# Moving the product that spreads the gates over rows to the bank of the first values, in the second cross attention of a two-layer gated block

## The chip, the cores and the metric

One core of a Trainium2 chip. The time is that of one execution on the device, in microseconds; the kernel before has a median of 4245.28 us over 3 runs (4242.39 to 4248.78).

## The reference

The program is a block of four parts on `x` (64 sequences of 64 rows of 128), in fp32. Each part adds its gated result to `x`; ahead of each stands a layer norm. The parts are a cross attention with memory slots, six layers of local attention and feed-forward, a second cross attention with gates, and a mixture of experts. The change lies in the third:

```python
attn = softmax(einsum('bhnd,bhmd->bhnm', q, k) * SCALE, axis=-1)
g = transpose(x @ w_la, (0, 2, 1))
gate = 0.5 * mean(g, axis=-1)[:, :, None, None] + 0.5 * max(g, axis=-1)[:, :, None, None]
attn2 = softmax(gate * attn, axis=-1)
attn = w * attn2 + (1.0 - w) * attn
out = einsum('bhnm,bhmd->bnhd', attn, v).reshape(B, N, C)
return out @ w_proj + b_proj
```

Here `x` is the context, and there are 16 heads of 8 columns. For each sequence and head there is one number `gate`. It multiplies a whole row of the first softmax, and what comes of that goes through a second softmax. Both softmaxes weigh the same values.

## The kernel before

The third part works on 32 tiles of 128 rows, two sequences each. It is a software pipeline: in one round an engine works for tile `a` on its projections, for `b` (the tile before) on its scores, for `c` on its first softmax, for `d` on its second, for `e_` on its second values and its output, and for `f` on the norm for the next part. Each engine runs its own list in program order (`l_body` in each engine's block), and semaphores tie the lists together. `past(engine, name, count)` makes an engine wait for a semaphore. TensorE, ScalarE, VectorE and GpSimd each have their own list. The names in the prediction:

- `turn(tile, k, h)`: four transpositions of half `h` of the exponentials, for the first (`k` = 0, into `pp`) or second softmax (`k` = 1, into `turn`). ScalarE copies them to SBUF (`l_C1`, `l_C2`), and `pv(tile, k)` multiplies them by the values into `po[k]`, 16 small products at line 1750, signalled by `l_P1` or `l_P2`. The 17th and 18th columns of each product are the sums of the softmax.
- The bank `pj[1]` is shared within a round by four things: the transposed inputs (`xsx`, line 1763), the turned sum `l_os` (line 1798), the projection by `lpj` (line 1802), and the gates' product (line 1811). Each has to wait until the reader of the one before is through.
- The gates' product: GpSimd writes the gates of a tile as rows that all hold the sequence's value (`l_gb`, signal `l_ga`, line 717), and TensorE multiplies them by the identity, so that each row gets the 16 gates of its sequence. VectorE multiplies them by the reciprocal of the softmax's sums (`l_c1`, line 1329), and GpSimd then multiplies the exponentials by them (the tile `qn`, line 739, signal `l_z`).
- VectorE adds the projection to `X` (line 1314, signal `l_res`), then takes the reciprocal, the maximum and sum of the next gates (`l_gm`), `l_c1`, and the second half of the subtraction of the first softmax (line 1264). Line 1334 writes the normalised `Y`.
- On GpSimd the sum of the weighted values (`oT`, line 721, waiting for VectorE's line 1278), the keys (`big`, line 727), the bias on `X` and the deviation (`rstd`) stand between one multiplication by the gates and the next.

Of the kernel before, what the change touches and what calls it, by code (L numbers as in the profile page):

```python
# [19 lines left out]
L1H, L1D = 16, 8  # L20
# [10 lines left out]
ALU = mybir.AluOpType  # L31
# [18 lines left out]
def build(nc, x, ctx, g_xattn, g_ffn, wq_w, wq_b, wk_w, wk_b, wv_w, wv_b, mk, mv, wo_w, wo_b,  # L50
# [3 lines left out]
    with ExitStack() as stack:  # L54
        def sb(name, shape, dt=F32):
            return stack.enter_context(nc.sbuf_tensor(name, shape, dt))
# [3 lines left out]
        def sem(name):  # L60
            if name not in sems:
                sems[name] = stack.enter_context(nc.semaphore(name))
            return sems[name]
# [7 lines left out]
        def const(name):  # L71
            a, n = CONSTS[name]
            return K[:, a:a + n]

        ident = const("ident")
# [81 lines left out]
        pj = [stack.enter_context(nc.psum_tensor(f"pj{i}", [P, 512], F32)) for i in range(2)]  # L157
# [3 lines left out]
        po = [stack.enter_context(nc.psum_tensor(f"po{i}", [P, 512], F32)) for i in range(2)]  # L161
# [45 lines left out]
        def bc(ap, n):  # L207
            return ap.unsqueeze(len(ap.shape)).broadcast_to(list(ap.shape) + [n])
# [30 lines left out]
        def by_head(v):  # L239
            return v.rearrange("p (j t) -> p j t", t=S)  # L240
# [10 lines left out]
        l_kq = [kT[:, 2 * i:2 * i + 2, :] for i in range(2)]  # L251
        l_pT = [[pT[:, h, :] for h in range(2)], [sqb[h] for h in range(2)]]
        l_out = [po[i][:, 0:144].rearrange("p (k c) -> p k c", c=18) for i in range(2)]
        l_gb = [oT[:, i, :] for i in range(2)]
        l_o1 = [oT[:, 2 + i, :] for i in range(2)]
        l_o2, l_os, l_oT = oT[:, 4, :], oT[:, 5, :], oT[:, 6, :]
# [3 lines left out]
        l_rc = sb("l_rc", [P, 2, L1H])  # L260
        l_rw = sb("l_rw", [P, 2, L1H])
        l_c1 = sb("l_c1", [P, 2, L1H])
# [18 lines left out]
        def past_waits(eng, name):  # L281

            eng.sem_inc(sem(name), 1)
# [98 lines left out]
        def head_start(eng, *names):  # L382

            for name in names:
                eng.sem_inc(sem(name), START)

        def past(eng, name, count):

            eng.wait_ge(sem(name), count + START)  # L389
# [189 lines left out]
        def _(pool):  # L579
            def rsqrt(i, n, name, count):  # L580

                nc.gpsimd.tensor_tensor(n_eps(i, n), n_var(i, n), eps1[:, 0:n], ALU.add).then_inc(sem(name), 1)
                past(pool, name, count + 1)
                nc.gpsimd.tensor_tensor(n_rstd(i, n), n_eps(i, n), nhalf[:, 0:n], ALU.pow).then_inc(sem(name), 1)
# [122 lines left out]
            def l_body(a, b, c, d, e_, f):  # L707
                if b:
                    k = b.par % 2
                    past(pool, "l_gs", b.g + 1)  # L710
                    nc.gpsimd.tensor_tensor(l_gm[:, k, :], l_gm[:, k, :], l_half[:, :], ALU.mult).then_inc(sem("l_g1"), 1)
                    pool.wait_ge(sem("l_g1"), b.g * 2 + 1)
                    nc.gpsimd.tensor_tensor(l_gm[:, k, 0:2], l_gm[:, k, 0:2], l_gm[:, k, 2:4], ALU.add).then_inc(sem("l_g1"), 1)
                    pool.wait_ge(sem("l_g1"), b.g * 2 + 2)
                    past(pool, "l_gr", b.g - 1)
                    past_waits(pool, "went_on")
                    nc.gpsimd.tensor_copy(l_gb[k].rearrange("p (b s) -> p b s", b=BT), bc(l_gm[:, k, 0:2], S)).then_inc(sem("l_ga"), 1)
                if e_:
                    past(pool, "l_t2", e_.g + 1)
                    past(pool, "l_oT", e_.g)  # L720
                    nc.gpsimd.tensor_tensor(l_os, l_o1[e_.par % 2], l_o2, ALU.add).then_inc(sem("l_os"), 1)
                if a:
                    past(pool, "l_kq", a.g + 1)
                    past(pool, "l_s", a.g - 1)
                    kk = l_kq[a.par % 2][:, 0, :].rearrange("p (b t) -> p b t", b=BT)
                    for bb in range(BT):
                        nc.gpsimd.tensor_tensor(l_km[a.par % 2][:, bb], kk[:, bb, :].unsqueeze(1).broadcast_to([P, L1HALF, S]),
                                                bc(const("headmask"), S), ALU.mult).then_inc(sem("l_km"), 1)
                if b:
                    nc.gpsimd.tensor_tensor(X[:, b.t, :], X[:, b.t, :], lpb[:, :], ALU.add).then_inc(sem("l_xb"), 1)  # L730
                if f:
                    past(pool, "norm_ag", f.g + (NT + NF + 1))
                    rsqrt(f.par, 1, "norm_nr", f.g * 2 + (2 * NT + 2 * NF))
                if c:
                    k = c.par % 2
                    past(pool, "l_c1", c.g + 1)
                    for h in range(2):
                        past(pool, "l_T2", c.g * 2 - 3 + h)
                        nc.gpsimd.tensor_tensor(by_head(l_e2[k][h]), by_head(l_e1[k][h]), bc(l_c1[:, k, L1HALF * h:L1HALF * h + L1HALF], S), ALU.mult).then_inc(sem("l_z"), 1)
# [5 lines left out]
            pool.wait_ge(sem("zeroed"), 3)  # L745
            pool.wait_ge(sem("l_la1"), 1)
            stream(pool, NT, l_body, 0, 0, 6, 4)


# [250 lines left out]
        def _(dve):  # L1000
# [253 lines left out]
            def l_body(a, b, c, d, e_, f):  # L1254
# [60 lines left out]
                if c:  # L1315
                    k = c.par % 2
# [7 lines left out]
                    nc.vector.tensor_reduce(l_gm[:, a.par % 2, 2:4], gv, AX, ALU.add).then_inc(sem("l_gs"), 1)  # L1324
                if c:
                    past(dve, "l_rc1", c.g * 2 + 1)
                    past(dve, "l_gr", c.g + 1)
                    past(dve, "l_z", c.g * 2 - 2)
                    nc.vector.tensor_tensor(l_c1[:, k, :], pj[1][:, 0:L1H], l_rc[:, k, :], ALU.mult).then_inc(sem("l_c1"), 1)
                    nc.vector.tensor_scalar(l_rw[:, k, :], l_rc[:, k, :], law[:, 1:2], None, ALU.mult).then_inc(sem("l_rc1"), 1)  # L1330
                sub1(1)
                if f:
# [91 lines left out]
        @block.tensor  # L1424
        def _(pe):
            mm = nc.tensor.matmul
            head_start(pe, "l_T", "l_pj", "l_s", "l_T1", "l_T2", "l_P1", "l_P2", "l_oT", "l_pr", "l_gr", "x_T", "x_ch", "x_s", "x_t", "x_pv", "x_wo", "d_xT", "d_ch", "d_vp", "d_tt", "d_s", "d_pt", "d_pv", "d_wo", "f_h", "f_y", "f_xnT")
            pe.wait_ge(s_ld, NLOAD)
            for i in range(2):
                if i:  # L1430
# [301 lines left out]
            def l_body(a, b, c, d, e_):  # L1732
# [9 lines left out]
                def pv(tile, k):  # L1742
                    if tile:
                        past(pe, "l_C%d" % (k + 1), tile.g * 2 + 2)
                        past(pe, "l_t%d" % (k + 1), tile.g)
                        past_waits(pe, "went_on")
                        for p in range(8):
                            for bb in range(BT):
                                q = slice(bb * 64, bb * 64 + 64)
                                last = mm(l_out[k][q, p, :], l_pT[k][p // 4][:, (p % 4) * P + bb * 64:(p % 4) * P + bb * 64 + 64],  # L1750
                                          l_vp[tile.par][:, bb, p, :], start=True, stop=True)
                        last.then_inc(sem("l_P%d" % (k + 1)), 1)
# [2 lines left out]
                turn(c, 0, 0)  # L1755
                if a:
                    pe.wait_ge(sem("l_in%d" % (a.par % 2)), a.half * 64 + (a.par // 2 * 32 + 32))
                    if d:
                        past(pe, "l_c1", d.g + 1)
                    else:  # L1760
                        past(pe, "l_xc", a.g)
                    for i in range(2):
                        last = nc.tensor.transpose(pj[1][:, i * P:i * P + P], xsx[:, a.par % 2, i, :], ident)
                    last.then_inc(sem("l_T"), 1)
# [25 lines left out]
                if e_:  # L1790
                    past(pe, "l_os", e_.g + 1)
                    if a:
                        past(pe, "l_xc", a.g + 1)
                    elif d:
                        past(pe, "l_c1", d.g + 1)
                    else:
                        past(pe, "l_res", e_.g)
                    nc.tensor.transpose(pj[1][:, 0:P], l_os, ident).then_inc(sem("l_oT"), 1)
                pv(c, 0)
                if e_:  # L1800
                    past(pe, "l_oc", e_.g + 1)
                    mm(pj[1][:, 0:D], l_oT, lpj[:, :], start=True, stop=True).then_inc(sem("l_pr"), 1)
                if c:
                    past(pe, "l_ga", c.g + 1)
                    if e_:
                        past(pe, "l_res", e_.g + 1)
                    elif a:
                        past(pe, "l_xc", a.g + 1)
                    else:
                        past(pe, "l_c1", c.g)  # L1810
                    mm(pj[1][:, 0:L1H], l_gb[c.par % 2][0:L1H, :], ident[0:L1H, 0:L1H], start=True, stop=True).then_inc(sem("l_gr"), 1)

            past(pe, "f_hT", DEPTH * (3 * NF))
            past(pe, "f_xT", DEPTH * NF)
# [118 lines left out]
```

## Time and profile before

| | us |
|---|---|
| median of 3 runs | 4245.28 |
| profiled execution | 4245.7 |
| its span, first to last instruction | 4243.9 |
| TensorE matmuls busy | 4020.4 (95%) |
| VectorE busy | 3504.6 (83%) |
| ScalarE busy | 2999.4 (71%) |
| GpSimd busy | 2867.3 (68%) |

The third part lies between about 3620 and 3997 us. Busy shares are means over the whole program and say little on one part, so the rows below are read in windows of that part. A timeline row gives the start in us from the span's beginning, the duration, engine, line, operation, what is written from what, and the count of merged instructions; a matmul in fp32 leaves two records.

### The profile page before, as it was taken

How to read it: one execution, taken by the hardware profiler on the slowest of the kernel's cores; microseconds unless marked ns; L12 is line 12 of the kernel's file. 1: busy time of each engine (PE TensorE's matmuls, PEld its weight loads, DVE VectorE, ACT ScalarE, POOL GpSimd, SP SyncE). 2: the span in 40 equal slices, each digit the busy share in tenths (PEclk: the TensorE clock that was granted, in tenths of full speed). 3: DMA queues.
4: the chain of work that ended last, by engine and by line, in shares of the span. 5: the costliest groups of instructions: out<-in, count | busy, mean ns of one | idle time of the engine just before them, and what ended most of it. 6: DMA issues, size and time to landing. Idle time of an engine off the chain costs nothing.

```text
span 4243.9 us, 147344 instructions
## 1 busy us (share of the span) xinstructions
PE 4020.4 (95%) x50345; PEld 2806.3 (66%) x50345; DVE 3504.6 (83%) x7236; ACT 2999.4 (71%) x6796; POOL 2867.3 (68%) x3647
## 2 busy tenths in 40 slices
PE   5999998999999999999999999999999998788799
PEld 3777775666666666666666666666666666566665
DVE  4666667999888998899988998899989998677566
ACT  2555556888888888788878887888888887554322
POOL 2333337888888888888887888788888887555200
PEclk9999999999999999999999999999999999887699
DMA  3000001000000001000000001000010000000000
GB/s 89 6 7 7 6 4 48 10 8 10 24 22 9 9 8 34 12 8 9 24 21 8 10 7 31 16 10 7 10 35 11 7 10 9 18 12 11 2 10 10
DMA packets 162227, 64.81 MB, mean 15 GB/s; under 512 B 121556, under 2 KB 156128, under 8 KB 162016
## 3 DMA queue, kind: packets, MB, share of 16 engines
q1 hardware_dynamic: 162016, 62.05, 5.8%
q8 instruction: 126, 2.06, 0.2%
q14 instruction: 85, 0.70, 0.1%
HBM read 26.54 MB, written 2.10 MB: 7 GB/s over the span
## 4 chain that ended last, share of the span: by engine, by line
POOL 43%; issue 25%; PE 24%; DVE 5%; POOLq 2%; SPq 1%; ACT 1%; DVEq 0%; DMA 0%; ACTq 0%
POOL qn L646 10%; POOL qn L635 8%; POOL big L646 7%; POOL e L641 5%; POOL big L635 4%; PE pj L1506 3%; PE pp L1464 2%; PE po L1479 2%; PE sc L1861 2%; PE pj L1498 2%; PE pj L1547 1%; POOL rstd L657 1%; PE po L1485 1%; POOLq L389 1%; PE turn L1450 1%
## 5 line engine op out<-in xcount | busy, mean ns | idle before, releaser
L1573 PE MATMUL pj<-wqkv,xcT 128*128 128x512 f32 x1536 | 799.5, 602 | 17.0 <-issue 9.2
L646 POOL TENSOR_TENSOR qn<-qn,big 128x512 f32<-128x512 f32 x384 | 490.5, 1278 | 289.9 <-DVE big L1139 289.9
L818 ACT ACTIVATE big<-pj 128x512 f32<-128x512 f32 x768 | 473.7, 617 | 69.0 <-PE pj L1573 59.2
L1139 DVE TENSOR_TENSOR big<-pj,ropes 128x512 f32<-128x512 f32 x768 | 521.3, 679 | 0.0
L1145 DVE TENSOR_REDUCE ss<-big 128x8 f32<-128x512 f32 x768 | 514.8, 671 | 0.1
L646 POOL TENSOR_TENSOR big<-big 128x512 f32<-128x512 f32 x384 | 485.1, 1273 | 4.7 <-DVE big L1139 4.7
L1726 PEld LDWEIGHTS pp<-wo,oT 128*128 128x128 f32 x3072 | 358.7, 192 | 161.7 <-issue 82.6
L641 POOL TENSOR_TENSOR e<-e,rc 128x512 f32<-128x512 f32 x384 | 400.2, 1042 | 55.7 <-DVE rc L1169 55.7
L635 POOL TENSOR_TENSOR qn<-qn,ny 128x512 f32<-128x512 f32 x384 | 396.7, 1043 | 7.5
L635 POOL TENSOR_TENSOR big<-big,ny 128x512 f32<-128x512 f32 x384 | 396.2, 1043 | 7.6
L1726 PE MATMUL pp<-wo,oT 128*128 128x128 f32 x3072 | 395.4, 282 | 2.3 <-ACT oT L841 1.2
L1580 PE MATMUL pj<-wqkv,xcT 128*64 128x512 f32 x1536 | 395.0, 614 | 0.7 <-DVE big L1139 0.6
L1138 DVE TENSOR_TENSOR qn<-pj,ropec 128x512 f32<-128x512 f32 x384 | 262.2, 683 | 134.5 <-ACT big L818 110.8
L861 ACT ACTIVATE e<-e 128x512 f32<-128x512 f32 x384 | 242.1, 631 | 116.5 <-DVE e L1158 114.4
L1138 DVE TENSOR_TENSOR big<-pj,ropec 128x512 f32<-128x512 f32 x384 | 263.6, 687 | 66.4 <-ACT big L818 60.2
L1663 PE MATMUL po<-f_xcT,fw 128*128 128x256 f32 (+1 forms) x1152 | 298.0, 382 | 1.5 <-DVE hT L1179 0.8
L1158 DVE TENSOR_TENSOR e<-sc,mx 128x512 f32<-128x512 f32 x384 | 265.5, 691 | 36.4
L1663 PEld LDWEIGHTS po<-f_xcT,fw 128*128 128x128 f32 (+1 forms) x1152 | 202.4, 180 | 114.5 <-issue 90.3
L1151 DVE TENSOR_REDUCE mx<-sc 128x8 f32<-128x512 f32 x384 | 260.4, 678 | 6.0 <-PE sc L1617 5.9
L1573 PEld LDWEIGHTS pj<-wqkv,xcT 128*128 128x128 f32 x1536 | 232.1, 191 | 45.6 <-DVE big L1139 27.2
L1163 DVE TENSOR_REDUCE sm<-e 128x8 f32<-128x512 f32 x384 | 259.4, 676 | 0.0
L612 POOL TENSOR_TENSOR e<-e,x_rc 128x384 f32<-128x384 f32 x128 | 105.7, 826 | 216.7 <-DVE x_rc L1064 216.7
(320 smaller groups left out, 9938.3 us busy)
## 6 DMA issues: line engine op xcount, KB each, us to landing
wqkv<-in_L_ffn_Wqkv SPq DMA_DIRECT2D x18, 512.0 KB, 3.7
xsd<-Y SPq DMA_DIRECT2D x192, 32.0 KB
xsd<-Y SPq DMA_DIRECT2D x384, 15.8 KB
xsf<-Y SPq DMA_DIRECT2D x96, 64.0 KB
xsf<-Y SPq DMA_DIRECT2D x192, 31.5 KB
xsx<-Y SPq DMA_DIRECT2D x64, 64.0 KB, 1.8
xsx<-CT SPq DMA_DIRECT2D x64, 64.0 KB, 1.9
wo<-in_L_ffn_Wo SPq DMA_DIRECT2D x6, 512.0 KB, 4.2
```

Of the source, the lines that this page charges most:

```text
L635: nc.gpsimd.tensor_tensor(uv, uv, bc(ny[:, tile.par, 8 * i:8 * i + 8], DK), ALU.mult).then_inc(sem("d_un"), 1)
L641: nc.gpsimd.tensor_tensor(ev, ev, bc(rc[:, p, 0:8], S), ALU.mult).then_inc(sem("d_pr"), 1)
L646: nc.gpsimd.tensor_tensor(U[a.par][i], U[a.par][i], t2b[i % 2], ALU.add).then_inc(sem("d_add"), 1)
L818: nc.scalar.activation(sqb[i % 2], pj[i % 2][:, :], ACT.Square).then_inc(sem("d_sq"), 1)
L1138: nc.vector.tensor_tensor(t1v, pv, cos, ALU.mult)
L1139: nc.vector.tensor_tensor(t2v, swapped, sin, ALU.mult).then_inc(sem("d_r"), 1)
L1145: nc.vector.tensor_reduce(ss[:, i, :], sqb[i % 2].rearrange("p (h d) -> p h d", d=DK), AX, ALU.add).then_inc(sem("d_ss"), 1)
L1158: nc.vector.tensor_tensor(e[:, p, :].rearrange("p (a t) -> p a t", t=S), sv, bc(mx[:, p, 0:8], S), ALU.subtract).then_inc(sem("d_sub"), 1)
L1573: mm(pj[i % 2][:, :], xcT[:, a.par, :], wqkv[:, i * 512:i * 512 + 512], start=True, stop=True).then_inc(sem("d_ch"), 1)
L1580: last = mm(pj[bb][a2 * 64:a2 * 64 + 64, :].rearrange("p (q c) -> p q c", c=2 * DK), xcT[:, a.par, bb * 64:bb * 64 + 64], wv[:, a2], start ...
L1663: last = mm(f_hid[j][0:m, (1 - k) * 256:(1 - k) * 256 + 256], fw1[:, k * FI + o:k * FI + o + m], f_xcT[:, :], start=True, stop=True)
L1726: last = mm(pp[:, 0:D], oT[:, k, :], wo[:, k, :], start=(k == 0), stop=(k == HP - 1))
```

## The change

The gates' product no longer goes to `pj[1]` at the end of a round but to 16 free columns of `po[0]`, directly ahead of the 16 products of the first values. It has no signal of its own (`l_gr` is gone): VectorE relies on `l_P1`, that of the values. Two waits are added at the head of the values, for `l_ga` and for `l_c1` of the tile before. The inputs' transpositions now wait for `l_res` of the last finished tile, as that is what last reads `pj[1]`. GpSimd waits for `l_P1` before it overwrites a gates buffer.

```diff
+        l_gates = po[0][:, 144:144 + L1H]
...
-                    past(pool, "l_gr", b.g - 1)
+                    past(pool, "l_P1", b.g - 1)
...
                     past(dve, "l_rc1", c.g * 2 + 1)
-                    past(dve, "l_gr", c.g + 1)
                     past(dve, "l_z", c.g * 2 - 2)
-                    nc.vector.tensor_tensor(l_c1[:, k, :], pj[1][:, 0:L1H], l_rc[:, k, :], ALU.mult).then_inc(sem("l_c1"), 1)
+                    nc.vector.tensor_tensor(l_c1[:, k, :], l_gates, l_rc[:, k, :], ALU.mult).then_inc(sem("l_c1"), 1)
...
                         past(pe, "l_C%d" % (k + 1), tile.g * 2 + 2)
                         past(pe, "l_t%d" % (k + 1), tile.g)
+                        if k == 0:
+                            past(pe, "l_ga", tile.g + 1)
+                            past(pe, "l_c1", tile.g)
                         past_waits(pe, "went_on")
+                        if k == 0:
+                            mm(l_gates, l_gb[tile.par % 2][0:L1H, :], ident[0:L1H, 0:L1H], start=True, stop=True)
                         for p in range(8):
...
-                    if d:
-                        past(pe, "l_c1", d.g + 1)
+                    if e_:
+                        past(pe, "l_res", e_.g)
                     else:
                         past(pe, "l_xc", a.g)
...
                     if a:
                         past(pe, "l_xc", a.g + 1)
-                    elif d:
-                        past(pe, "l_c1", d.g + 1)
                     else:
                         past(pe, "l_res", e_.g)
                     nc.tensor.transpose(pj[1][:, 0:P], l_os, ident).then_inc(sem("l_oT"), 1)
...
-                if c:
-                    past(pe, "l_ga", c.g + 1)
-                    if e_:
-                        past(pe, "l_res", e_.g + 1)
-                    elif a:
-                        past(pe, "l_xc", a.g + 1)
-                    else:
-                        past(pe, "l_c1", c.g)
-                    mm(pj[1][:, 0:L1H], l_gb[c.par % 2][0:L1H, :], ident[0:L1H, 0:L1H], start=True, stop=True).then_inc(sem("l_gr"), 1)
```

On TensorE, from the turned sum of one round to the inputs' transpositions of the next, the kernel before has these instructions in a round of the loop (`K` is the tile that holds the identity, `oT` holds `l_os`, `l_oT` and the gates):

```order
L1798 MATMUL pj<-K,oT 128x128 [waits l_xc,l_os]
L1750 MATMUL po<-big,pT 64x18 [waits l_C1,l_t1]
L1750 MATMUL po<-big,pT 64x18 x15
L1802 MATMUL pj<-lpj,oT 128x128 [waits l_oc]
L1811 MATMUL pj<-K,oT 128x16 [waits l_res,l_ga]
L1739 MATMUL turn<-K,qn 128x128 [waits l_C2,l_ex2]
L1739 MATMUL turn<-K,qn 128x128 x3
L389 REGISTER_ALU
L1739 MATMUL pp<-K,e 128x128 [waits l_C1,l_ex1]
L1739 MATMUL pp<-K,e 128x128 x3
L1757 REGISTER_ALU
L1763 MATMUL pj<-K,xsx 128x128 [waits l_c1,l_in0]
```

The changed kernel has, at the same place and up to those transpositions:

```order
L1801 MATMUL pj<-K,oT 128x128 [waits l_xc,l_os]
L1751 MATMUL po<-K,oT 128x16 [waits l_c1,l_ga,l_C1,l_t1]
L1755 MATMUL po<-big,pT 64x18 x16
L1805 MATMUL pj<-lpj,oT 128x128 [waits l_oc]
L1739 MATMUL turn<-K,qn 128x128 [waits l_C2,l_ex2]
L1739 MATMUL turn<-K,qn 128x128 x3
L390 REGISTER_ALU
L1739 MATMUL pp<-K,e 128x128 [waits l_C1,l_ex1]
L1739 MATMUL pp<-K,e 128x128 x3
L1762 REGISTER_ALU
L1768 MATMUL pj<-K,xsx 128x128 [waits l_res,l_in0]
```

The gates' product has gone from behind the projection, where it waited for `l_res`, to the head of the first values. The wait for `l_res` now stands at the inputs' transpositions, two blocks of turns later.

On VectorE, the kernel before has this from the addition to `X` to the second subtraction (`l_c` is `l_c1`):

```order
L1314 TENSOR_TENSOR X<-pj,X 128x128
L1318 RECIPROCAL l_rc<-po 128x16 [waits l_P1]
L389 REGISTER_ALU
L1323 TENSOR_REDUCE l_gm<-pj 128x2 [waits l_ga,l_kq]
L1324 TENSOR_REDUCE l_gm<-pj 128x2
L1329 TENSOR_TENSOR l_c<-pj,l_rc 128x16 [waits l_z,l_gr,l_rc1]
```

The changed kernel has there:

```order
L1315 TENSOR_TENSOR X<-pj,X 128x128
L1319 RECIPROCAL l_rc<-po 128x16 [waits l_P1]
L390 REGISTER_ALU
L1324 TENSOR_REDUCE l_gm<-pj 128x2 [waits l_ga,l_kq]
L1325 TENSOR_REDUCE l_gm<-pj 128x2
L1329 TENSOR_TENSOR l_c<-po,l_rc 128x16 [waits l_z,l_rc1]
```

The order is the same; `l_c1` reads another bank and has one wait less.

## Rows read from the trace of the kernel before

**Rows 1.** The page's 40 equal slices of the span: TensorE's granted clock in tenths.
```profile
PEclk9999999999999999999999999999999999887699
```

**Rows 2.** The windows view of the part's middle and end.
```profile
core 0: us, PE busy (x) PEld busy (x) DVE busy (x) ACT busy (x) POOL busy (x), PEclk, DMA share, GB/s
3661.00:3956.00 295.00, 251.22 (x2949) 193.76 (x2948) 219.54 (x569) 152.94 (x352) 169.38 (x300) 0.83 0.04 11
3956.00:3996.00 40.00, 26.81 (x261) 20.41 (x260) 19.41 (x55) 13.00 (x27) 11.75 (x23) 0.59 0.00 1
```

**Rows 3.** Timeline of GpSimd, the multiplications by the gates.
```profile
3661.38 2.04 POOL L739 TENSOR_TENSOR qn<-e,l_c 128x512 f32<-128x512 f32 x2
...
3760.05 2.04 POOL L739 TENSOR_TENSOR qn<-e,l_c 128x512 f32<-128x512 f32 x2
...
3770.08 2.04 POOL L739 TENSOR_TENSOR qn<-e,l_c 128x512 f32<-128x512 f32 x2
...
3800.35 2.04 POOL L739 TENSOR_TENSOR qn<-e,l_c 128x512 f32<-128x512 f32 x2
...
3812.02 2.04 POOL L739 TENSOR_TENSOR qn<-e,l_c 128x512 f32<-128x512 f32 x2
...
3822.62 2.04 POOL L739 TENSOR_TENSOR qn<-e,l_c 128x512 f32<-128x512 f32 x2
...
3833.33 2.04 POOL L739 TENSOR_TENSOR qn<-e,l_c 128x512 f32<-128x512 f32 x2
...
3846.93 2.04 POOL L739 TENSOR_TENSOR qn<-e,l_c 128x512 f32<-128x512 f32 x2 [0.45 <-DVE l_c L1329]
...
3955.98 2.04 POOL L739 TENSOR_TENSOR qn<-e,l_c 128x512 f32<-128x512 f32 x2
```

**Rows 4.** Waits from 3661 to 3956: us together, times, longest.
```profile
POOL oT L721 <- DVE oT L1278: 86.4, 27, 4.8
PE pj L1798 <- POOL oT L721: 20.3, 26, 1.3
PE pj L1811 <- DVE X L1314: 19.3, 27, 0.7
DVE mx L1258 <- PE sc L1774: 9.0, 11, 1.6
DVE l_r L1298 <- PE po L1750: 8.8, 21, 1.1
DVE Y L1334 <- POOL rstd L584: 6.1, 24, 0.3
DVE l_c L1329 <- PE pj L1811: 2.2, 6, 0.4
```

**Rows 5.** Timeline of TensorE, a round at full clock.
```profile
3767.21 0.49 PE L1802 MATMUL pj<-lpj,oT 128*128 128x128 f32 x2
3768.42 0.36 PE L1811 MATMUL pj<-K,oT 16*128 16x16 f32 x2 [0.72 <-DVE X L1314]
3768.71 0.66 PE L1739 MATMUL turn<-K,qn 128*128 128x128 f32 x4
...
3770.69 1.09 PE L1774 MATMUL sc<-big,kbuf 64*64 64x512 f32 x8
```

**Rows 6.** Timeline of TensorE, the same place at the low clock.
```profile
3797.51 0.80 PE L1802 MATMUL pj<-lpj,oT 128*128 128x128 f32 x2
3799.03 0.58 PE L1811 MATMUL pj<-K,oT 16*128 16x16 f32 x2 [0.72 <-DVE X L1314]
3799.54 1.11 PE L1739 MATMUL turn<-K,qn 128*128 128x128 f32 x4
```

**Rows 7.** Timeline of VectorE, the same full-clock round.
```profile
3769.29 0.68 DVE L1264 TENSOR_TENSOR e<-sc,mx 128x512 f32<-128x512 f32 x1
3770.24 0.97 DVE L1334 TENSOR_SCALAR Y<-X,dif,rstd  x1 [0.27 <-POOL rstd L584]
```

**Rows 8.** The chain that ended last, in a round of the tail.
```profile
3964.10 0.30 DVE X L1314
...
3964.54 0.57 PE pj L1811 x2
```

More of the change, by code:

```diff
@@ L1426, in _ @@
             mm = nc.tensor.matmul
-            head_start(pe, "l_T", "l_pj", "l_s", "l_T1", "l_T2", "l_P1", "l_P2", "l_oT", "l_pr", "l_gr", "x_T", "x_ch", "x_s", "x_t", "x_pv", "x_wo", "d_xT", "d_ch", "d_vp", "d_tt", "d_s", "d_pt", "d_pv", "d_wo", "f_h", "f_y", "f_xnT")
+            head_start(pe, "l_T", "l_pj", "l_s", "l_T1", "l_T2", "l_P1", "l_P2", "l_oT", "l_pr", "x_T", "x_ch", "x_s", "x_t", "x_pv", "x_wo", "d_xT", "d_ch", "d_vp", "d_tt", "d_s", "d_pt", "d_pv", "d_wo", "f_h", "f_y", "f_xnT")
             pe.wait_ge(s_ld, NLOAD)
```

## The prediction

> **What bounds the kernel now.** I read the page first. Its slices show TensorE busy nearly everywhere, and the granted clock, full almost throughout, lower at slices 35 to 38 of 40 [rows 1], 3607 to 4032 us. The edit touches only the second cross attention, 3620 to 3997 us, so the rest of the program is left out. The windows view of 295 us of that stage gives 251.22 us of busy TensorE at a mean granted clock of 0.83, a mixture of its two levels of 1.2 and 2.4 GHz, and the stage's last 40 us stand at 0.59 [rows 2].
>
> Next I took the length of a round, from one GpSimd multiply by the gates (`qn`) to the next. From 3661.38 to 3955.98 us stand 28 such starts, so 27 rounds in 294.60 us, 10.91 us each. At full clock a round takes 3770.08 - 3760.05 = 10.03 us, and none of the steady ones is shorter; the others take 10.60 (3812.02 to 3822.62), 11.67 (3800.35 to 3812.02) or, in the worst case, 13.60 (3833.33 to 3846.93) [rows 3]. The 27 rounds are 6 within 0.2 us of 10.03 (0.35 us above it together), 11 that are 0.42 to 0.74 us above (6.1 together) and 10 that are 0.87 to 3.57 us above (17.3 together): 23.8 us in all.
>
> What sets 10.03 is a ring through GpSimd and VectorE. GpSimd waits 86.4 us, in all 27 rounds, for the second weighted values of VectorE [rows 4], then sums them, TensorE turns the sum, ScalarE copies it and the keys, GpSimd builds the keys, adds the bias, takes the deviation and multiplies. TensorE has only the one turn in that ring. It gets into it otherwise when it is late: 21 times VectorE waited 8.8 us together for the second values (`l_r`, L1298), 11 times 9.0 us for the scores [rows 4]. So the 23.8 us are what a late TensorE costs, and it is late when its clock is at 1.2 GHz.
>
> Last, what TensorE waits for. In every round it stands between the projection and the gates' product, for the addition to `X` on VectorE: 19.3 us over 27 rounds [rows 4]. At full clock the projection starts at 3767.21 and is through at 3767.70, the gates' product stands at 3768.42, the next round's first turn at 3768.71 [rows 5].
>
> **The change part by part.** Per round it moves one matmul (two records), swaps its waits, and takes one wait off VectorE.
>
> *Removed:* the turns no longer stand behind the addition to `X`. From the end of the projection to the next round's first turn it is now 3768.71 - 3767.70 = 1.01 us at full clock, and 3799.54 - 3798.31 = 1.23 us at the low one (3797.51 + 0.80) [rows 5, 6]. That falls to nothing: the operands of the turn are an exponential that ScalarE has by then, while the `xsx` turns, which still need `l_res` (of the tile before) because they overwrite `pj[1]`, come after two blocks of turns. The next round's scores were also behind; they start at 3770.69.
>
> *Added ahead of the projection:* the gates' product, 3768.71 - 3768.42 = 0.29 us at full clock, 3799.54 - 3799.03 = 0.51 at the low one [rows 5, 6]. Net advance of TensorE's next round: 1.01 - 0.29 = 0.72 in both cases (1.23 - 0.51 = 0.72). Since a following block starts a little before the modelled end of the one before (3768.71 against 3768.42 + 0.36 = 3768.78), some 0.1 us more comes of it, while two more waits at the head of the values take a little. I take 0.80 us. The lower bound is where the scores meet their own wait for VectorE's last subtraction, 3769.29 + 0.68 = 3769.97, and about 0.14 us of signal: 3770.11, an advance of 0.58 [rows 5, 7]. The upper bound is 1.01, if the product hides behind the turn of the sum ahead of it.
>
> The Trainium skill prices the product a little lower: TensorE: Matmul & The Clock Gate, section LDWEIGHTS, gives the columns over 1.2 GHz, an estimate of 0.107 us for each of the two loads, so 0.21 us. By it ten rounds and the tail would gain 0.08 us more each, about 1 us in all; the sum here goes by the row's 0.29.
>
> *What the delay of the projection costs:* the addition to `X` comes 0.29 us (0.51) later plus issue. Behind it on VectorE stand the reciprocal, two reductions of the gates, `l_c1`, `l_rw`, a subtraction and the normalisation of `Y`, which waited for GpSimd's deviation 24 times, 6.1 us together [rows 4], 0.25 us each; `l_c1` loses its wait for the gates' product, which is last in 6 of the rounds and costs 2.2 us there [rows 4]. At full clock the subtraction ends at 3769.97 and `Y` begins at 3770.24 [rows 7], so 0.27 us of cover against 0.29 less the 0.1 to 0.2 that `l_c1` stood: nothing. If the issue of the waits adds 0.1 or more, the 27 rounds pay at most 0.1 each, 2.7 us. I take nothing, and keep 2.7 for the range.
>
> *GpSimd* waits for `l_P1` of the tile two before instead of `l_gr`; it is a round old. `l_ga`, `l_c1` of the last tile and `l_t1` are past as well when the values begin. `l_c1` now reads from the bank of the values, after `l_P1`, which VectorE had waited for already.
>
> *Sum:* the 6 clean rounds gain nothing, since the ring sets them. The 11 rounds that are 0.42 to 0.74 above give back all, 6.1 us. The 10 long ones give 0.80 each, 8.0. The tail has three rounds with no keys to build, where the chain that ended last goes projection, `X` (0.30), gates' product (0.57), turns [rows 8]; 3 x 0.80 = 2.4. Together 16.5 us. By the bounds: 5.7 + 5.8 + 1.7 - 2.7 = 10.5 (5.7 is what 0.58 leaves of the 11), and 6.1 + 9.8 + 3.0 = 18.9. The profiled execution took 4245.7 us (span 4243.9), 0.4 above the median of 4245.28; 4245.7 - 16.5 = 4229.2, and I forecast 4229.
>
> **The rivals.**
>
> *The clock stays up (chance 0.12).* What made TensorE slow was in each case a stretch at 1.2 GHz. If a shorter round keeps it at 2.4, every round goes to 10.03: 23.8 + 2.4 = 26.2 us, 4219. For it: five rounds in a row of before did so. Against: idle time per round stays the same or grows.
>
> *The addition to X takes the place of the wait (0.16).* The projection is later, and where the clock is low by 0.51 us plus issue; cover is 0.27. Then the long rounds gain 0.80 but pay 0.24 to 0.4 of it on VectorE, and the 11 middle ones gain about half: 3 + 10 x 0.4 + 1.5 = 8.5, less up to 2.7 in the others: 4237 to 4240. For it: behind `X` VectorE has no gap at full clock but those two. Against: `Y` then waits for GpSimd nearly always.
>
> *Nothing is given back (0.05).* The ring through GpSimd takes all; 4243 to 4246. The 8.8 and 9.0 us of waits for TensorE [rows 4] speak against it.
>
> *The clock falls more (0.07), the case that is slower.* Two gaps of TensorE in a round, before the turn of the sum and before the gates' product (20.3 and 19.3 us over 27 rounds [rows 4]), become one of about 1.5 us or more. If that makes more stretches at 1.2 GHz, rounds go towards the 13.60 of the round that stood at it throughout; with 0.80 off it, 12.80. Between 10.03 at 2.4 GHz and 12.80 at 1.2, a mean clock that is 0.1 lower costs 0.55 us a round, 15 us in 27. So from 0.83 the gain is gone at about 0.72, and below 0.66 it is slower by over 8.5 us; all at the low level would give 27 x 12.80 against 294.60, 51 us more, 4297.
> The Trainium skill has a rule for this side: TensorE: Matmul & The Clock Gate, section HAM oscillation, says that the array falls back to the slow clock when idle stretches between bursts are long, and that it takes work without gaps to get it back. By it a merged gap is worse than two. That the clock falls in rounds with such gaps agrees with the 0.83 here; that a merged one is worse no row of before shows.
>
> **How the numbers follow.** The forecast has 0.60, with its own range of 4224 to 4235. 0.2% is 8.5 us, about what a measurement of this kernel can tell from no change, so the bound is 4236.8. Faster: 0.60 + 0.12 and a little of the second rival, 0.74. Same: 0.19, the second and third rivals. Slower: 0.07. The range of 4219 to 4241 takes in the clean clock and the late `X`, and leaves out the slower case and the edges.
>
> **What the changed profile would show.** The wait of TensorE for `DVE X` is gone, and the gap before the turn of the sum is larger. The product for the gates stands ahead of the 16 products of the values, with 0.3 us to the next. Full-clock rounds stay at 10.0 us; those with one slow stretch come near it; the worst are below 13 us. The reciprocal of the second values waits under 5 us for them, and `l_c1` for nobody. The prediction is wrong if clean rounds are longer than 10.1 us (then `X` was on the ring), if the mean clock of the stage is under 0.78, or if the long rounds are no shorter.

## The result, and the profile after

The changed kernel takes 4229.90 us (median of 5 runs, 4227.25 to 4232.62), beside 4248.78 for the kernel before (5 runs, 4242.39 to 4255.10). The ratio is 0.9949, 95% interval 0.9936 to 0.9961: 0.5% faster. The profiled execution has a span of 4225.4 us, 18.5 less than that of before.

The windows view of the changed kernel, same stretches as in [rows 2]:

```profile
3661.00:3956.00 295.00, 244.99 (x3081) 189.41 (x3075) 221.36 (x596) 160.55 (x369) 175.54 (x310) 0.88 0.04 11
3956.00:3996.00 40.00, 31.85 (x210) 28.97 (x208) 11.29 (x32) 6.71 (x13) 5.08 (x10) 0.50 0.00 1
```

The clock of the middle went from 0.83 to 0.88, and TensorE's busy time from 251.22 to 244.99 us although more rounds fall into the window. The second stretch stands at 0.50 throughout; the part ends at 3978.2 in this execution, so some of that stretch lies behind it.

GpSimd's multiplications by the gates (timeline; line 740 is the old 739), as in [rows 3]:

```profile
3659.95 2.04 POOL L740 TENSOR_TENSOR qn<-e,l_c 128x512 f32<-128x512 f32 x2
...
3754.09 2.04 POOL L740 TENSOR_TENSOR qn<-e,l_c 128x512 f32<-128x512 f32 x2
...
3764.12 2.04 POOL L740 TENSOR_TENSOR qn<-e,l_c 128x512 f32<-128x512 f32 x2
...
3938.29 2.04 POOL L740 TENSOR_TENSOR qn<-e,l_c 128x512 f32<-128x512 f32 x2
```

There are 28 starts from 3659.95 to 3938.29, as there were 28 in [rows 3]. So 27 rounds take 278.34 us, 10.31 each, where they took 294.60, 10.91 each: 16.3 us. A full-clock round is 3764.12 - 3754.09 = 10.03 us, unchanged. Sixteen rounds now lie within 0.22 us of it (6 before), ten are 0.31 to 0.81 above (before, 11 from 0.42 to 0.74), and one is 1.13 above (10 by 0.87 or more). Of 23.8 us above the ring 7.5 are left.

The waits from 3661 to 3956, as in [rows 4]:

```profile
POOL oT L722 <- DVE oT L1279: 73.8, 29, 3.5
PE pj L1801 <- POOL oT L722: 44.5, 29, 3.1
DVE X L1315 <- POOL X L731: 16.1, 5, 3.3
POOL qn L740 <- DVE l_c L1329: 5.8, 6, 3.4
DVE Y L1334 <- POOL rstd L585: 5.6, 21, 0.3
DVE l_r L1299 <- PE po L1755: 2.4, 7, 0.6
DVE mx L1259 <- PE sc L1779: 0.5, 1, 0.5
```

TensorE's wait for the addition to `X` is gone; the one before the turn of the sum grew from 20.3 to 44.5 us. VectorE waits 2.4 us for the second values (8.8 before) and 0.5 for the scores (9.0). New is that GpSimd waits for `l_c1` 6 times, 5.8 us together: 3.37 of it at 3948.65, where the tail begins, and 2.4 in five of the 27 rounds, 0.35 to 0.53 each (before, one of the 27 rounds had such a wait, 0.45 [rows 3]). One of the five, with the addition to `X` ahead of it:

```profile
3742.51 0.29 DVE L1315 TENSOR_TENSOR X<-pj,X 128x128 f32 x1 [3.25 <-POOL X L731]
3743.54 2.04 POOL L740 TENSOR_TENSOR qn<-e,l_c 128x512 f32<-128x512 f32 x2 [0.53 <-DVE l_c L1329]
```

In these rounds the projection stands at the low clock (0.80 us at 3741.43, below) and is through at 3742.23, together with GpSimd's bias on `X`; they are the five waits of `X L1315` for GpSimd above.

TensorE in a round that began at the low clock and in the next, as in [rows 5, 6]:

```profile
3741.43 0.80 PE L1805 MATMUL pj<-lpj,oT 128*128 128x128 f32 x2
3742.01 1.06 PE L1739 MATMUL turn<-K,qn 128*128 128x128 f32 x4
...
3749.83 0.33 PE L1801 MATMUL pj<-K,oT 128*128 128x128 f32 x1 [0.66 <-POOL oT L722]
3750.09 0.39 PE L1751 MATMUL po<-K,oT 16*128 16x16 f32 x2
3750.41 1.11 PE L1755 MATMUL po<-big,pT 128*64 128x18 f32 x32
3751.45 0.49 PE L1805 MATMUL pj<-lpj,oT 128*128 128x128 f32 x2
3751.78 0.60 PE L1739 MATMUL turn<-K,qn 128*128 128x128 f32 x4
...
3754.12 1.09 PE L1779 MATMUL sc<-big,kbuf 64*64 64x512 f32 x8 [0.34 <-DVE e L1265]
```

At full clock the projection starts at 3751.45 and the turn of the next round at 3751.78, 0.33 us later where it was 1.50 [rows 5]. At the low clock it is 3742.01 - 3741.43 = 0.58, where it was 2.03 [rows 6]. The gates' product takes 3750.41 - 3750.09 = 0.32 us ahead of the values.

What the advance is worth shows in two rounds whose scores took the same time, partly at the low clock. Before, in the round of 11.67 us from 3800.35 [rows 3]:

```profile
3802.72 1.71 PE L1774 MATMUL sc<-big,kbuf 64*64 64x512 f32 x8
3804.50 0.69 DVE L1258 TENSOR_REDUCE mx<-sc 128x8 f32<-128x512 f32 x1 [1.13 <-PE sc L1774]
```

and in the changed kernel, in a round of 10.04 us from 3774.16:

```profile
3774.81 1.72 PE L1779 MATMUL sc<-big,kbuf 64*64 64x512 f32 x8
3777.10 0.68 DVE L1259 TENSOR_REDUCE mx<-sc 128x8 f32<-128x512 f32 x1
```

The scores start 2.37 us after GpSimd's multiplication there and 0.65 here. VectorE waited 1.13 us for them there and not at all here. Not all of the 1.7 us is the change's: the low clock also set in earlier in the round of before, at its projection.

To compare the part by itself I take, in each profiled execution, the time from the turn of the last small router weight (`egw`) to the start of the last normalised tile `Y`, and the 27 rounds above. The parts are good to 0.1 us. What comes before the part varies by 19 us over the profiled executions of these kernels (`egw` starts between 3619.8 and 3638.7 us), none of which touches it, and what comes after takes 246.3 to 247.8 us in all. For the kernel before the part is 3997.5 - 3625.5 = 372.0 us, for the changed one 3978.2 - 3622.9 = 355.3: a gain of 16.7. "Clock" is the mean granted clock from 3661 to 3956 us; in the faster kernels that takes in a piece of the tail, and over its own 27 rounds the changed kernel has 0.89, once more 0.88, and the one with the product in the gap 0.83. Part, round and clock are of one execution each. Each ratio is to the kernel before run beside that kernel; its medians there were 4253.24 us for the wait kept, the product in the gap, three products and the gap's two fills, 4250.36 for "once more", "before, gap filled", one fill and three fills, 4246.97 for the last two rows, and 4246.64 for five products. So medians of different groups differ by up to 7 us for no reason of the kernel's.

| kernel | ratio to before (95%) | median us | part us | round us | clock |
|---|---|---|---|---|---|
| before | 1 | 4248.78 | 372.0 | 10.91 | 0.83 |
| changed | 0.9949 (0.9936 to 0.9961) | 4229.90 | 355.3 | 10.31 | 0.88 |
| changed, once more | 0.9955 (0.9940 to 0.9971) | 4231.47 | 352.0 | 10.18 | 0.86 |
| changed, wait for `X` kept | 1.0010 (0.9998 to 1.0022) | 4256.72 | 383.9 | 11.26 | 0.78 |
| product in the gap | 0.9959 (0.9944 to 0.9974) | 4233.12 | 355.4 | 10.28 | 0.83 |
| three products | 0.9952 (0.9937 to 0.9968) | 4231.44 | 356.7 | 10.26 | 0.85 |
| five products | 1.0017 (1.0008 to 1.0026) | 4252.53 | 374.3 | 10.98 | 0.81 |
| before, gap filled (2) | 0.9952 (0.9937 to 0.9968) | 4231.66 | 352.8 | 10.28 | 0.96 |
| product in the gap, 1 fill | 0.9959 (0.9944 to 0.9974) | 4233.36 | 352.7 | 10.23 | 0.93 |
| product in the gap, 2 fills | 0.9933 (0.9915 to 0.9952) | 4223.06 | 343.2 | 10.11 | 0.97 |
| product in the gap, 3 fills | 0.9940 (0.9926 to 0.9953) | 4225.10 | 343.0 | 10.09 | 1.00 |
| the same once more | 0.9949 (0.9932 to 0.9967) | 4225.82 | 347.4 | 10.12 | 0.99 |
| changed, 3 fills | 0.9955 (0.9940 to 0.9970) | 4229.03 | 347.8 | 10.22 | 0.94 |

One of the twelve executions with the wait kept took 12918.37 us; the row leaves it out.

### The profile page after: what moved, and what is told of

Its sections match the earlier page's. It is cut to its first block, busy times and chain, and to the rows that moved or that the text cites. A ratio compares the mean times of both kernels' runs of the same rounds, so it can differ in the third digit from the quotient of the medians.

```text
span 4225.4 us, 147330 instructions
## 1 busy us (share of the span) xinstructions
PE 4006.7 (95%) x50345; PEld 2796.1 (66%) x50345; DVE 3495.9 (83%) x7236; ACT 2999.8 (71%) x6796; POOL 2867.5 (68%) x3647
## 4 chain that ended last, share of the span: by engine, by line
POOL 45%; issue 26%; PE 21%; DVE 5%; POOLq 2%; SPq 1%; ACT 1%; DVEq 0%; DMA 0%; ACTq 0%
POOL qn L647 11%; POOL qn L636 8%; POOL big L647 7%; POOL e L642 6%; POOL big L636 4%; PE pj L1506 3%; PE pp L1464 2%; PE po L1479 2%; PE sc L1855 2%; PE pj L1498 2%; PE pj L1547 1%; POOL rstd L658 1%; PE po L1485 1%; POOL qn L740 1%; POOLq L390 1%
```

## The experiments

The theory: the gain is that TensorE goes on with the next round without waiting for the addition to `X`, and this saves time where its clock is at 1.2 GHz, since only then is it late for the ring through GpSimd and VectorE. The rivals: that VectorE no longer waits for the product; that the new place of the product matters by itself; that the clock alone made the difference, and the order does nothing.

### The wait kept

Behind the projection of the changed kernel:

```diff
                     mm(pj[1][:, 0:D], l_oT, lpj[:, :], start=True, stop=True).then_inc(sem("l_pr"), 1)
+                if c and e_:
+                    past(pe, "l_res", e_.g + 1)
```

> The changed kernel, but TensorE still waits for the addition to X behind the projection (the gates' product stays at its new place). If the gain comes from TensorE going on without that wait, nearly all of it goes: 4241 to 4250 us, about the kernel before or up to 3 us above it, since the product now delays the projection too. If it comes from VectorE no longer waiting for the product, or from where the product stands, the time stays near 4230.

It took 4256.72 us, ratio 1.0010 (0.9998 to 1.0022): the whole gain is gone. The time is above the 4241 to 4250 expected, beside 4253.24 for the kernel before on that chip. A wait (from 3680 to 3960 us) and the window of this kernel:

```profile
PE turn L1739 <- DVE X L1315: 20.3, 25, 1.2
```

```profile
3661.00:3956.00 295.00, 255.28 (x2870) 195.52 (x2870) 206.39 (x545) 149.04 (x343) 163.20 (x286) 0.78 0.04 11
```

The wait is back (20.3 us, 25 times, against 19.3, 27 times, in a window of 295 us [rows 4]), rounds take 11.26 us, and the clock is down at 0.78. The product's new place and the wait that VectorE lost are both still in this kernel, so neither is the gain. Its part is 12 us longer than before's in one execution each. The product, which now delays the projection too, may have a share in that, and the lower clock too; no run parts them, and by the ratios no difference from before can be told.

### The product in the gap

The product goes ahead of the wait for the weighted sum:

```diff
+                if c:
+                    past(pe, "l_ga", c.g + 1)
+                    past(pe, "l_c1", c.g)
+                    past(pe, "l_t1", c.g)
+                    mm(l_gates, l_gb[c.par % 2][0:L1H, :], ident[0:L1H, 0:L1H], start=True, stop=True)
                 if e_:
                     past(pe, "l_os", e_.g + 1)
```

and is taken out of `pv`.

> The gates' product goes one step further forward, into the idle gap ahead of the turn of the weighted sum, behind a wait for the first weighted values of the tile before. It then delays neither the projection nor X. If the late addition to X costs something in the rounds with a slow stretch, this is 2 to 5 us faster than the changed kernel (4225 to 4228). If the cover on VectorE holds everywhere, it is the same within 1 us.

It took 4233.12 us, ratio 0.9959 (0.9944 to 0.9974), part 355.4 us: the same as the changed kernel, so the 0.32 us that the product costs the projection cost nothing that can be measured. GpSimd's five waits for `l_c1` are not there in its 27 rounds, and the mean round of 10.28 us is no different from 10.31 all the same. That is the second of the two cases, though the median lies above both ranges.

This run also speaks to the last rival. Its clock is 0.83, that of the kernel before, also over its own 27 rounds, and its rounds are 10.28 us where those of before are 10.91. So the new order gains at the same mean clock; a better clock isn't needed for it.

### Three and five products

```diff
-                            mm(l_gates, l_gb[tile.par % 2][0:L1H, :], ident[0:L1H, 0:L1H], start=True, stop=True)
+                            for _ in range(3):
+                                mm(l_gates, l_gb[tile.par % 2][0:L1H, :], ident[0:L1H, 0:L1H], start=True, stop=True)
```

> The changed kernel with the gates' product made three times over ahead of the values (same output): 0.6 us more at full clock, 1.0 at the low one, ahead of the projection. If the addition to X has only some 0.2 us of cover left, each round pays about 0.3 to 0.6 us, 9 to 16 us together: 4239 to 4246. If TensorE's order alone matters and X has ample cover, only the long rounds pay, under 4 us.

It took 4231.44 us, ratio 0.9952 (0.9937 to 0.9968). The delay was made (TensorE's timeline in that kernel; 0.77 us from the first product to the values):

```profile
3780.99 0.84 PE L1752 MATMUL po<-K,oT 16*128 16x16 f32 x6
3781.76 1.11 PE L1756 MATMUL po<-big,pT 128*64 128x18 f32 x32
```

That is 0.45 more than the 0.32 of one, not 0.64. But the rounds are 10.26 us, 20 of 27 within 0.22 of 10.03. Eleven of these 20 are 0.08 to 0.12 above it, where 12 of the 16 of the changed kernel are within 0.02, so some 0.1 us a round may be the price at full clock; it doesn't show in the time. The first case, 9 to 16 us, did not come: the cover of `X` is larger than the 0.27 us that I had read. VectorE and GpSimd in a round of this kernel show where it is (first row GpSimd, then the normalisation of `Y` and the next reduction):

```profile
3784.91 2.04 POOL L740 TENSOR_TENSOR qn<-e,l_c 128x512 f32<-128x512 f32 x2
...
3785.39 0.65 DVE L1334 TENSOR_SCALAR Y<-X,dif,rstd  x1
3785.99 0.69 DVE L1270 TENSOR_REDUCE mx<-qn 128x8 f32<-128x512 f32 x1
```

`Y` begins 0.48 us after GpSimd's multiply here, 0.16 after it in [rows 3, 7], and ends at the same distance: 3785.39 + 0.65 - 3784.91 = 1.13, and 3770.24 + 0.97 - 3770.08 = 1.13. Its duration had a wait in it. More on that below.

The same with `range(5)`:

> The changed kernel with the gates' product made five times over ahead of the values (same output), 4 x 0.32 = 1.28 us more at full clock. In the changed kernel the multiplier for GpSimd is ready 0.85 us before GpSimd takes it, and the normalisation of Y, which begins 0.28 us after VectorE is free, is prolonged to 0.97 us where it takes 0.34 alone. If those 0.85 to 0.9 us are the cover of the addition to X, a full-clock round gets 0.35 to 0.45 us longer, 10.4 to 10.5, and the time is 4238 to 4250. If only the 0.28 us of idle time are cover, it gets 1.0 us longer, 11.0, and the time is above 4252.

It took 4252.53 us, ratio 1.0017 (1.0008 to 1.0026), rounds of 10.98 us. By its time it is just in the second case, with a mean round just below its 11.0. But the five products take about 1.20 us to the values (3740.93 - 3739.72 = 1.21 in one round, 3751.51 - 3750.33 = 1.18 in the next), so the extra was 0.88 and not 1.28 us; by the first case a full-clock round would then hardly grow, by the second it would by 0.6. The shortest rounds are 10.58 to 10.60, 0.55 above 10.03, yet the clock was at 0.81, and slow stretches lie in these rounds too, so they don't tell. GpSimd waited for `l_c1` 17 times, 12.1 us together. So an extra delay of 0.45 us costs nothing measurable and one of 0.88 costs over 20 us in 32 rounds, all the gain; where at full clock it begins to cost is not settled.

### The gap filled, with the old order and the new

The kernel before, with work for TensorE in its gap ahead of the turn of the sum; what the two products compute is read by nobody:

```diff
+                if c:
+                    past(pe, "l_t1", c.g)
+                    for _ in range(2):
+                        mm(po[0][:, 256:512], ident, K[:, 0:256], start=True, stop=True)
                 if e_:
                     past(pe, "l_os", e_.g + 1)
```

> The kernel before, untouched but for two products of 256 columns, read by nobody, in TensorE's gap ahead of the turn of the sum. If the wait for X costs time only through the stretches at the low clock, keeping the clock up is worth nearly as much as the change: the rounds come near 10.03 us and the time to 4222 to 4236. If the wait costs time at full clock as well, rounds stay above 10.4 us and the time above 4240. If the fill does not keep the clock up, it is slower than before, 4250 to 4270.

It took 4231.66 us, ratio 0.9952 (0.9937 to 0.9968), the gain of the change without the change. TensorE in a full-clock round of it, and the window:

```profile
3793.94 1.13 PE L1793 MATMUL po<-K 128*128 128x256 f32 x4
3795.32 0.33 PE L1802 MATMUL pj<-K,oT 128*128 128x128 f32 x1 [0.25 <-POOL oT L721]
...
3796.62 0.49 PE L1806 MATMUL pj<-lpj,oT 128*128 128x128 f32 x2
3797.84 0.36 PE L1815 MATMUL pj<-K,oT 16*128 16x16 f32 x2 [0.73 <-DVE X L1314]
3798.13 0.66 PE L1739 MATMUL turn<-K,qn 128*128 128x128 f32 x4
```

```profile
3661.00:3956.00 295.00, 259.56 (x3216) 197.49 (x3217) 231.14 (x602) 161.90 (x371) 178.55 (x312) 0.96 0.04 11
```

TensorE still waits 0.73 us for `X` and still starts its turns 1.51 us after the projection, but with a clock of 0.96 twenty of 27 rounds are within 0.25 of 10.03 us. The wait costs nothing at full clock. So the theory holds in both its halves, and the third rival in one: a better clock alone gives the same gain, as the old order is slow only through the low clock. That the order then does nothing is refuted by the product in the gap, which gained at the clock of before. The new order makes TensorE late less often at a clock that is still low for a good part.

The same with the product in the gap, and one, two or three fills:

```diff
                     mm(l_gates, l_gb[c.par % 2][0:L1H, :], ident[0:L1H, 0:L1H], start=True, stop=True)
+                    for _ in range(2):
+                        mm(po[0][:, 256:512], ident, K[:, 0:256], start=True, stop=True)
```

> As the kernel with the product in the gap and two filling products, with one instead of two (0.43 us). If the clock falls for lack of work in that part of the round, this lies between none and two: clock of the stage 0.86 to 0.95, time 3 to 7 us below the changed kernel or equal to two. If the fill must be whole to count, it is as without any, within 2 us of the changed kernel.

> The product in the gap, and behind it two more products of 256 columns into unused columns of the same bank, whose result nobody reads: about 0.9 us of work in TensorE's gap. If the slow stretches come from that gap and set what is left above 10.03 us per round, the mean granted clock of the stage rises from 0.88 to over 0.95 and the time falls by 4 to 9 us against the kernel with the product in the gap. If the clock has nothing to do with the gap, the time is the same or up to 10 us longer, since at the low clock the filling takes 1.7 us of a shorter gap.

> Three filling products (1.3 us) where two left about 0.9 us of idle time. If there is room at full clock and the clock then never falls, rounds of 10.03 to 10.1 us and 0 to 3 us below the kernel with two. If a slow stretch catches the fill (2.6 us in a gap of under 2), single rounds get longer by up to 1 us, and it is 1 to 6 us above.

They took 4233.36, 4223.06 and 4225.10 us. The windows of one, two and three fills:

```profile
3661.00:3956.00 295.00, 253.78 (x3200) 192.44 (x3193) 223.37 (x605) 160.82 (x375) 178.39 (x316) 0.93 0.04 12
```

```profile
3661.00:3956.00 295.00, 259.46 (x3289) 195.84 (x3285) 227.15 (x614) 161.76 (x375) 180.81 (x316) 0.97 0.04 12
```

```profile
3661.00:3956.00 295.00, 267.90 (x3366) 203.39 (x3366) 228.37 (x612) 163.12 (x380) 182.17 (x318) 1.00 0.04 12
```

The clock goes from 0.83 with none to 0.93, 0.97 and 1.00, and the rounds from 10.28 to 10.23, 10.11 and 10.09 us. With the same two fills the old order had 10.28 at a clock of 0.96 and a part of 352.8 us against 343.2 here; 5.7 of these 9.6 us lie in the tail, where the clock is low in both (0.54). With three there is 0.38 us of the gap left:

```profile
3789.90 0.39 PE L1794 MATMUL po<-K,oT 16*128 16x16 f32 x2
3790.22 1.56 PE L1796 MATMUL po<-K 128*128 128x256 f32 x6
3792.16 0.33 PE L1803 MATMUL pj<-K,oT 128*128 128x128 f32 x1 [0.38 <-POOL oT L722]
```

The tail gains more than the rounds: its last two come to 8.58 and 7.99 us, where they were 9.48 and 12.16 before and 10.36 and 10.47 in the changed kernel. One fill gained nothing in the time (4233.36 beside 4231.47 for the changed kernel on that chip), neither of the two cases that I had for a clock of 0.86 to 0.95. Two were 10.1 us faster than the product in the gap without a fill (4233.12 on the same chip), more than the 4 to 9 expected; three are the same as two by the ratios.

> The changed kernel as it is, as a measure on this chip for the others: ratio 0.994 to 0.996 to the kernel before, rounds of 10.2 to 10.4 us in the profile, mean granted clock of the stage 0.85 to 0.90.

On the chip of one and three fills the changed kernel had 4231.47 us, ratio 0.9955 (0.9940 to 0.9971), part 352.0 us, as expected.

### The change with the fills, and the three fills once more

> The changed kernel with the gates' product where the change put it, ahead of the values, and three filling products in TensorE's gap. At full clock the product delays X by 0.3 us, and the kernel with three products ahead of the values had about 0.1 us more per round for 0.6. So with the clock at 1.00 the rounds are 10.03 to 10.1 us, and the time is that of the kernel with the product in the gap and three fills, 4222 to 4230. If the place of the product matters at full clock, it is over 3 us slower.

> The kernel with the product in the gap and three fills once more, beside the former on the same chip: ratio 0.993 to 0.995 to the kernel before, rounds of 10.05 us, 4222 to 4230.

4229.03 us, ratio 0.9955 (0.9940 to 0.9970), and 4225.82 us, ratio 0.9949 (0.9932 to 0.9967). The rounds are 10.22 and 10.12 us, where 10.03 to 10.1 and 10.05 were expected. The premise of the first was not met: with the product ahead of the values the clock reached only 0.94.

```profile
3661.00:3956.00 295.00, 278.48 (x3330) 210.81 (x3328) 227.18 (x607) 163.79 (x375) 178.16 (x312) 0.94 0.04 12
```

So the place of the product was not tried there at a full clock. Side by side it is 3.2 us slower than the product in the gap, with eleven rounds 0.28 to 0.48 above 10.03 where that one has two over 0.22, but the ratio intervals overlap, and the clock is a rival cause. The profiled parts of the new order with two or three fills, 343.0 to 347.8 us, are shorter than those of the changed one, 352.0 and 355.3; the medians of the four are 0.9 to 8.4 us below the changed kernel's two, and the ratio intervals overlap. That a fill beats the change is likely by the profiles and is not shown by the times.

## Why the prediction was right

**The size.** Forecast 4229, measured 4229.90; the forecast gain was 16.5 us from a profiled execution of 4245.7, the measured one 18.9 between medians and 16.7 in the part. The kernel before came out 3.5 us slower over five runs than over three, so a part of the agreement in absolute time is luck. So is the closeness of 16.7 to 16.5: a second execution of the changed kernel has a part of 352.0, which would make it 20.0, and the kernel before was profiled once. That the gain lies in the rounds, and that it is TensorE's advance, is not luck.

**The advance of TensorE (0.80 us a round).** Measured from the start of the projection to the next turn it is 1.50 - 0.33 = 1.17 at full clock, less 0.32 for the product: 0.85; at the low one 2.03 - 0.58 = 1.45, less the product's 0.5 there [rows 6]: 0.94. The wait at the scores that set my lower bound is there (0.34 us for VectorE's subtraction at 3754.12), but only where the scores run at full clock (1.09 us), in rounds with little or nothing to gain.

**Which rounds gain.** Forecast: clean 0, middle ones all, long ones 0.80 each, 14.1 in 27 rounds. Measured 16.3, with 7.5 of 23.8 us left where I had 9.7. The rounds can't be paired, since the slow stretches fall elsewhere in each execution.

**The tail (2.4 us).** From the last of the 28 starts to the last `Y` it was 3997.5 - 3955.98 = 41.5 us and is 3978.2 - 3938.29 = 39.9: 1.6. The filling of the pipeline, which I had at nothing, got longer: 3661.38 - 3625.5 = 35.9 before, 3659.95 - 3622.9 = 37.1 now.

**The cover of X.** Right in its result, wrong in its working: I had 0.27 us of cover against 0.29, and kept 2.7 us for it. Three products show that 0.45 us more cost nothing measurable. The step that failed is that I took a busy VectorE for a working one. Where the projection stands at the low clock the cover was not enough: GpSimd waited for `l_c1` in five rounds, 2.4 us together, inside the 2.7 kept and up to a third of the 7.5 us that are left.

**The rivals.** The late addition to `X` did not come as priced: it took 0.35 to 0.53 us in five rounds and not half of the gain, and with the product in the gap, where it is gone, the time is the same. As a cost of most rounds it sets in only from an extra delay between 0.45 and 0.88 us. Nothing given back is refuted by the result. The clock did not fall: 0.88 for 0.83, although the two gaps did become one, and TensorE's longest idle stretch within the 27 rounds went from 1.30 to 2.14 us. The Trainium skill's rule on idle stretches (TensorE: Matmul & The Clock Gate, section HAM oscillation) agrees in its direction with the fills, which took the clock from 0.83 to 1.00; that a merged gap is worse than two no run shows, and the clocks of before and changed kernel speak against it. The clock that stays up, which I gave 0.12, came about with the fills alone: 343.0 us for the part, 29 less than before, where I had put 26.2.

## What to carry to other kernels

Where a ring of other engines sets a round, look at which rounds are above the ring's time and what the clock of TensorE was in them: the wait to take away is the one that makes a slow TensorE late, even if it costs nothing at full clock. A bank of PSUM that four results share chains engines that have nothing else to do with each other; moving the smallest of them into free columns of a bank that is written at the same moment, under the signal of what follows, takes a link out. And before an idle gap of TensorE is called harmless, try it with work that nobody reads: in the kernel before that alone gave 0.5%.

## What the runs showed of the hardware

The normalisation of `Y` (one operand from SBUF, 128 x 128) takes 0.34 us when GpSimd does nothing, as in the tail of the kernel before:

```profile
3995.69 0.34 DVE L1334 TENSOR_SCALAR Y<-X,dif,rstd 128x128 f32<-128x128 f32 x1
```

and mostly 0.63 to 0.97 us when it begins just behind a GpSimd multiplication (two of 1.04 us each, merged into one row of 2.04). In all thirteen profiles, and in every round with such a multiplication, it ends 1.11 to 1.14 us after the start of the first one, wherever it began: 0.16 after it ([rows 3, 7]), 0.48 (three products), and in the kernel with five products 0.50:

```profile
3743.78 2.04 POOL L740 TENSOR_TENSOR qn<-e,l_c 128x512 f32<-128x512 f32 x2
...
3744.28 0.63 DVE L1334 TENSOR_SCALAR Y<-X,dif,rstd  x1
```

I read this as VectorE standing still inside the instruction until GpSimd's first multiplication is through, while the profile counts it as busy. The Trainium skill says so: SBUF — State Buffer, section Terms, has a pair of ports that the two engines share under a lock, held for the whole instruction, and the loser blocks. These rows agree with it.

The clock of a stretch with all its work unchanged followed what stood in one gap of each round: 0.83 with no fill in it, 0.93 with one product of 256 columns, 0.97 with two and 1.00 with three (the product in the gap and its fills, windows above; one execution each, and 0.99 for three fills once more). No long idle stretch is needed for the low clock: in the 27 rounds of the kernel before none is over 1.30 us, and its mean clock is 0.83. Without a fill it was:

```profile
3661.00:3956.00 295.00, 259.50 (x3114) 199.70 (x3115) 220.11 (x598) 160.23 (x371) 177.76 (x311) 0.83 0.04 11
```
